# The scan's decay, spreading and carried products placed side by side in parts of TensorE's array, with banks in pairs for ScalarE and VectorE and new orders of the steps

## The reference

```python
h = _layernorm(h, ln_w, ln_b)
z, xBC, dt = split(h @ in_w.T, [512, 512 + 640])          # dt: 8 heads
dt = softplus(dt + dt_bias)
xBC = silu(causal_depthwise_conv(xBC, conv_w) + conv_b)   # 4 taps
x, B, C = split(xBC, [512, 576])                          # 8 heads x 64; state size 64
dA = exp(-exp(A_log) * dt)
# per token: state = dA * state + (dt * x) B^T ;  y = state C
y = y + D * x
y = y * silu(z)
y = y * rsqrt(mean(y * y) + EPS) * rms_w
h = res + y @ out_w.T
```

## Time and profile before

| | us |
|---|---|
| median of three runs | 1965.81 |
| the profiled execution | 1965.04 |
| its span in the trace | 1963.3 |
| TensorE busy | 1815.8 |
| VectorE busy | 1445.5 |
| ScalarE busy | 1309.1 |
| GpSimd busy | 1173.3 |

### The profile page before, as it was taken

The page is one execution under the profiler, slowest core; times in us unless marked ns, Lnnn a source line. Parts: engine busy times, 40 slices in busy tenths (PEclk is TensorE's granted clock), DMA queues, the critical chain, the costliest instruction groups (busy, mean ns, idle before and its releaser), DMA issues. The chain is left out here.

```text
span 1963.3 us, 36509 instructions
## 1 busy us (share of the span) xinstructions
PE 1815.8 (92%) x12544; PEld 1378.9 (70%) x12544; DVE 1445.5 (74%) x3135; ACT 1309.1 (67%) x2317; POOL 1173.3 (60%) x1032
## 2 busy tenths in 40 slices
PE   5799999999999999999999999999986589899998
PEld 4577777677777777776777777767754478777786
DVE  4687788887877777777777777777743586878755
ACT  3677767777677767677767776777640467676675
POOL 2466666666666654555555555555540487877785
PEclk8899999999999999999999999999986799999999
DMA  4011111111111111111111111110104202121001
GB/s 142 23 38 39 39 37 48 59 37 43 37 37 37 37 39 38 44 58 47 43 37 37 37 37 37 48 59 27 33 12 149 86 1 92 38 76 55 22 22 44
DMA packets 87272, 91.97 MB, mean 47 GB/s; under 512 B 4928, under 2 KB 82448, under 8 KB 87184
## 3 DMA queue, kind: packets, MB, share of 16 engines
q1 hardware_dynamic: 79360, 79.46, 12.5%
q10 hardware_dynamic: 7824, 11.37, 2.4%
HBM read 57.26 MB, written 25.17 MB: 42 GB/s over the span
## 5 line engine op out<-in xcount | busy, mean ns | idle before, releaser
L860 POOL TENSOR_TENSOR L_xc<-L_xpad,L_vec 128x512 f32<-128x512 f32 x160 | 165.9, 1037 | 421.2 <-ACT L_xpad L659 394.0
L381 PE MATMUL L_front<-L_uhi,L_whi 128*128 128x512 f32 x576 | 247.2, 429 | 13.1 <-DVE L_xc L1078 8.4
L530 PE MATMUL L_mix<-L_wo,L_yg 128*128 128x256 f32 x1024 | 238.4, 387 | 3.2 <-POOL L_yg L852 3.2
L381 PE MATMUL L_front<-L_uhi,L_wlo 128*128 128x512 f32 x576 | 229.5, 398 | 0.0
L381 PE MATMUL L_front<-L_ulo,L_whi 128*128 128x512 f32 x576 | 229.5, 398 | 0.0
L1090 DVE TENSOR_TENSOR L_m<-L_dbank,L_gm 128x512 f32<-128x512 f32 x256 | 175.5, 686 | 69.0 <-ACT L_dbank L699 68.6
L530 PEld LDWEIGHTS L_mix<-L_wo,L_yg 128*128 128x128 f32 x1024 | 191.8, 192 | 34.7 <-issue 7.0
L852 POOL TENSOR_TENSOR L_yg<-L_yg,L_sz 128x512 f32<-128x512 f32 x128 | 164.0, 1281 | 86.1 <-DVE L_yg L1105 86.1
L659 ACT ACTIVATE L_xpad<-L_front,L_pbias 128x512 f32<-128x512 f32 x160 | 108.7, 680 | 132.4 <-PE L_front L381 131.6
L697 ACT ACTIVATE L_dbank<-L_dbank 128x512 f32<-128x512 f32 x256 | 148.8, 581 | 45.5 <-PE L_dbank L437 45.4
L487 PE MATMUL L_ybank<-L_m,L_dtx 128*64 128x128 f32 x2048 | 161.3, 284 | 5.5 <-DVE L_m L1090 5.5
(11 more groups left out here) (172 smaller groups left out, 4850.3 us busy)
## 6 DMA issues: line engine op xcount, KB each, us to landing
h<-L_hres SPq DMA_DIRECT2D x32, 512.0 KB, 3.0
L_hin<-in_x SPq DMA_DIRECT2D x16, 512.0 KB, 4.6
L_hres<-in_x SPq DMA_DIRECT2D x16, 512.0 KB, 3.8
L_cc<-L_xc ACTq DMA_DIRECT2D x64, 128.0 KB, 2.3
L_hin<-h SPq DMA_DIRECT2D x16, 512.0 KB, 4.7
L_hres<-h SPq DMA_DIRECT2D x16, 512.0 KB, 3.7
M_hin<-h SPq DMA_DIRECT2D x16, 512.0 KB, 4.7
M_xin<-in_x SPq DMA_DIRECT2D x16, 512.0 KB, 5.7
```

The costliest lines, as they stand in the source:

```text
L381: last = nc.tensor.matmul(to[:, :], ww[:, kd, tile * P:(tile + 1) * P], a[:, kd, :], start=i == 0, stop=i == len(passes) - 1)
L530: last = nc.tensor.matmul(mix[1 - s][:, (b % 2) * DM:(b % 2 + 1) * DM], yg[:, t, b * P:(b + 1) * P], wo[layer][:, t, :], start=t == 0, sto ...
L860: nc.gpsimd.tensor_tensor(xc[p][:, q, :].rearrange("p (b i) -> p b i", b=NB), xpad[:, q, :, 0:P], vector(layer, "conv_w", q * TAPS, 1).uns ...
```

## The change

The two decay banks become one tensor `dbank` of two banks, and the two `mix` banks are views of one tensor `both`.

- `decays(n, k)`, k = 0 to 3 over pair of sequences and half of the heads, makes two products: the pair's two sequences lie in different rows of the array and go to different banks. `exp_decay` and `weigh` then take both banks (1024 columns) in one instruction.
- `carry(n, pair)` makes four products of 64 rows by 64 columns, in four quarters of the array; `exp_carry` and `scale_c` take both banks in one. To suit this, the halves of `cs`, `sdecay` and `state` hold the heads in another order (`on_half`: heads 0, 3 of each four in the lower partitions, 1, 2 in the upper), and `sel` shrinks to 64 columns.
- `outputs(n, p, pair)` makes two output tiles: `within` of both, then `carried` of both, in which four consecutive products (two tiles by odd and even head) lie in four quarters of the array and, by row, in different banks.
- The step sizes' weights get a tensor `wdt` of their own with both parts beside each other, 16 output rows: four products instead of six; `bias_dt` adds the two parts in two instructions.
- `step` is written anew for TensorE, ScalarE, GpSimd and VectorE.
- `clear_halo`'s wait moves to `set_halo`.

```diff
             def project_dt(n):
...
-                passes = [(kd, a, ww) for kd in range(KD) for ww, a in ((whi, uhi), (whi, ulo), (wlo, uhi))]
-                for i, (kd, a, ww) in enumerate(passes):
-                    last = nc.tensor.matmul(front[0][0:NH, :], ww[:, kd, NPROJ - NH:NPROJ], a[:, kd, :],
+                passes = [(kd, a) for kd in range(KD) for a in (uhi, ulo)]
+                for i, (kd, a) in enumerate(passes):
+                    last = nc.tensor.matmul(front[0][0:2 * NH, :], wdt[:, kd, :, :].rearrange("p i h -> p (i h)"), a[:, kd, :],
...
-            def decays(n, q):
-                b, half = q // 2, q % 2
+            def decays(n, k):
+                pair, half = k // 2, k % 2
...
-                wait(pe, m_done, 8 * n + q - 1)
-                rows = slice(ROWS * (b % 2), ROWS * (b % 2) + ROWS)
-                nc.tensor.matmul(dbank[half][:, :], dstat[rows, b // 2, :],
-                                 dmov[rows, b // 2, 4 * half:4 * half + 4, :], start=True, stop=True).then_inc(d_ready, 1)
+                wait(pe, m_done, 4 * n + k)
+                for i in range(2):
+                    rows = slice(ROWS * i, ROWS * i + ROWS)
+                    last = nc.tensor.matmul(dbank[:, i, :], dstat[rows, pair, :], dmov[rows, pair, 4 * half:4 * half + 4, :], start=True, stop=True)
+                last.then_inc(d_ready, 1)
...
+            def carry(n, pair):
+                scaled_x, kept_b, scaled_c = known(pe, NB * n + 4), known(pe, n + 1), known(pe, 2 * n + 1)
+                pe.wait_ge(consts_ready, 3)
+                if pair == 0:
+                    pe.wait_ge(dtx_done, scaled_x)
+                    pe.wait_ge(bt_done, kept_b)
                 else:
+                    pe.wait_ge(cs_done, scaled_c)
+                moving = dmov[:, pair, :, :].rearrange("r (k f) i -> r k f i", f=4)
+                for half in range(2):
+                    for i in range(2):
+                        rows = slice(ROWS * i, ROWS * i + ROWS)
+                        last = nc.tensor.matmul(mix[i][HD * half:HD * half + HD, :], sel[rows, :], moving[rows, :, on_half(half), :],
+                                                start=True, stop=True)
                 last.then_inc(ec_ready, 1)
...
             def carried(n, p, t, b):
                 for odd in range(2):
                     half = slice(HD * odd, HD * odd + HD)
-                    made = nc.tensor.matmul(ybank[t % 2][half, b * P:(b + 1) * P], state[p][half, b, t, :], cs[half, b, t, :],
+                    rows = slice(HD, 2 * HD) if (odd + t) % 2 else slice(0, HD)
+                    made = nc.tensor.matmul(ybank[t % 2][half, b * P:(b + 1) * P], state[p][rows, b, t, :], cs[rows, b, t, :],
...
+            def outputs(n, p, pair):
+                first, second = 2 * pair, 2 * pair + 1
+                if pair == 0:
+                    pe.wait_ge(m_done, 4 * n + 4)
+                for t in (first, second):
+                    wait(pe, y_skip, T * n + t - 1)
+                    for b in range(NB):
+                        within(n, t, b)
+                if pair == 0:
...
+                for b in range(NB):
+                    last_first = carried(n, p, first, b)
+                    last_second = carried(n, p, second, b)
+                last_first.then_inc(y_ready, 1)
+                last_second.then_inc(y_ready, 1)
...
+            def exp_decay(n, k):
+                act.wait_ge(d_ready, 4 * n + k + 1)
+                nc.scalar.activation(dbank[:, :, :], dbank[:, :, :], ACT.Abs).then_inc(d_abs, 1)
+                act.wait_ge(d_abs, 4 * n + k + 1)
+                nc.scalar.activation(dbank[:, :, :], dbank[:, :, :], ACT.Exp, scale=-1.0).then_inc(d_exp, 1)
...
+            def scale_c(n, pair):
+                dve.wait_ge(ec_exp, 2 * n + pair + 1)
+                of = cc[:, 2 * pair * P:(2 * pair + 2) * P].rearrange("p (b i) -> p b i", b=2)
+                nc.vector.tensor_tensor(cs[:, 2 * pair:2 * pair + 2, :, :], both[:, :, :].rearrange("p b (t i) -> p b t i", t=T),
+                                        of.unsqueeze(2).broadcast_to([P, 2, T, P]), ALU.mult).then_inc(cs_done, 1)
```

More of the change, by code:

```diff
@@ L40 @@
 NPROJ = 2 * DI + 2 * NS + NH
+NMAIN = NPROJ - NH
 SEQ, LEN = 8, 1024
@@ L241, in mamba_layers @@
         front = [bank(f"front{i}") for i in range(2)]
-        dbank = [bank(f"dbank{i}") for i in range(2)]
+        dbank = ctx.enter_context(nc.psum_tensor("L_dbank", [P, 2, 512], F32))
         ybank = [bank(f"ybank{i}") for i in range(2)]
-        mix = [bank(f"mix{i}") for i in range(2)]
+        both = ctx.enter_context(nc.psum_tensor("L_mix", [P, 2, 512], F32))
+        mix = [both[:, i, :] for i in range(2)]
         staged = m[:, :, :, :].rearrange("p b h i -> p (b h i)")[:, 0:C_END - C_MASK]
@@ L457, in turn_b @@
                 last.then_inc(bt_turned, 1)
[L459 to L464, removed]
-                else:
-                    pe.wait_ge(cs_done, NB * n + b - 1)
-                rows = slice(ROWS * (b % 2), ROWS * (b % 2) + ROWS)
-                moving = dmov[rows, b // 2, :, :].rearrange("r (t o) i -> r t o i", o=2)
-                for odd in range(2):
-                    last = nc.tensor.matmul(mix[b % 2][:, :], sel[rows, odd, :], moving[:, :, odd, :], start=odd == 0, stop=odd == 1)
+            def carry(n, pair):
[4 more added lines that the diff above has]
+                    pe.wait_ge(bt_done, kept_b)
+                else:
+                    pe.wait_ge(cs_done, scaled_c)
[5 more added lines that the diff above has]
+                                                start=True, stop=True)
                 last.then_inc(ec_ready, 1)
             def new_state(n, s):
-                pe.wait_ge(cs_done, NB * n + 3 + s)
+                pe.wait_ge(cs_done, 2 * n + 2)
                 pe.wait_ge(wx_done, NB * n + 2 * s + 2)
@@ L477, in new_state @@
                 for b in (2 * s, 2 * s + 1):
-                    values = wx[:, b, :, :].rearrange("p (t o) d -> p t o d", o=2)
-                    for odd in range(2):
-                        last = nc.tensor.matmul(mix[s][HD * odd:HD * odd + HD, (b % 2) * T * HD:(b % 2 + 1) * T * HD],
-                                                bt[:, b, :], values[:, :, odd, :], start=True, stop=True)
+                    values = wx[:, b, :, :].rearrange("p (k f) d -> p k f d", f=4)
+                    for half in range(2):
+                        last = nc.tensor.matmul(mix[s][HD * half:HD * half + HD, (b % 2) * T * HD:(b % 2 + 1) * T * HD],
+                                                bt[:, b, :], values[:, :, on_half(half), :], start=True, stop=True)
                 last.then_inc(st_ready, 1)
@@ L612, in step @@
                     fold_bias(layer_of(n, layer, 2))
+                result(n, layer, 0)
+                if more:
+                    decays(n + 1, 1)
                 if more2:
@@ L1225, in step @@
                     clear_halo(n, p)
-                skip(n, layer, p, 3)
                 if more:
-                    mask_scores(n + 1)
                     weigh(n + 1, 0)
-                    weigh(n + 1, 1)
                 if starts_layer(n + 2):
                     fold_rows(layer2)
+                mean_square(n)
                 if more2:
@@ L1235, in step @@
                     rest_u(n + 2, 1)
-                mean_square(n)
-                if more:
-                    weigh(n + 1, 2)
                 finish(n, layer, c, p, 0)
```

259 lines of the change are left out of this document (115 added, 144 removed).

## The result

The changed kernel takes 2000.61 us (median of 4 runs, 1999.91 to 2001.23), the kernel before 1965.87 beside it: ratio 1.0174, 95% interval 1.0162 to 1.0186. It is slower by 35 us. Forecast was 1909, and 2000.61 lies outside the range given. The profiled execution has a span of 1997.0 us against 1963.3.

The account below looks back on a forecast made before the run. TensorE was taken as the bound, with VectorE limiting the gain: 43.90 us per item to 42.1, 31x1.8 = 55.8 saved. 1965.0-55.8+1.4 (border)-2 (first and last item) = 1908.6, so 1909 us; range 1882 to 1948.

Parts of the forecast that it names:

- The rates: Times per product or operation on TensorE, VectorE and ScalarE, such as 0.12 us per four carried products.
- rival 1: TensorE's array quarters don't run side by side: no faster than two products per 0.11 us, about 1961 us; 7%.
- my floor of 41.4: Item time in us from laying rows end to end, without sum_da's last wait; 42.0 with it, 42.1 taken.
- the walk: One item's rows laid end to end in program order, each starting when engine and operand are free: 42.0 us.
- my own count of TensorE alone: TensorE's item without its waits: 43.9-0.85-4.8 = 38.3 us.
- Of 4.8 us some 1.8 are left: Of TensorE's 4.8 us relief per item, 1.8 shorten the item; the rest turns into waits for VectorE.
- the path: The new order of one item across the engines, pieces end to end with their waits, ending at 42.0 us.
- finish_dt to 38.2, so sum_da waits 0.6: Late in the item VectorE ends the step sizes at 38.2 us, so TensorE's sum_da waits 0.6.
- GpSimd's moved work (decay_state, ...) fits in its free 14 us: On GpSimd, decay_state, sums of squares and layer_norm ahead of the second tap fit in 14 free us per item.
- rival 3: Granted clock falls inside items where TensorE waits 1 us at a time: 45.3 us per item, 2008 us; 4%.
- the longer wait of the bias products (1.4): At the layer border, bias products ahead of result wait for ssq 2.7 us instead of 1.33: +1.4 once.
- A price of 0.46 per us of low clock: On TensorE each us of low clock costs 0.46; 7 us per item cost 3.2.

Follow-up runs that it names:

- both repairs: Changed kernel with finish_dt ahead of skip 0 and, at the layer border, fold_bias behind result half 0 and decays 1: 1873.46 us, ratio 0.953.
- the first experiment: Changed kernel with one move, VectorE's finish_dt ahead of skip 0 instead of behind skip 1, where GpSimd is idle: 1885.2 us, ratio 0.958.
- the filled wait: Changed kernel with four extra unused products on TensorE in front of its wait for da: 1950.88 us, ratio 0.9916.

## Why the prediction was wrong

*What held.* The rates. Two decay products at once, 0.39; four spreading products within 0.41; carried products start four within 0.02 us and the next four 0.109 later (taken: 0.12), so rival 1 is out. ScalarE's 1024-wide Exp takes 1.008 us (1.0), VectorE's product 1.223 (1.21). TensorE waits 1.04 for the last weighting (1.3), 1.03 for a convolution (0.95), 0.2 for the step sizes (0.3). One wait I had not seen: 0.57 for keep_b's copy ahead of the spreading. With the hold removed the item takes 40.95 us against my floor of 41.4 without the last wait and 42.1 with it: the walk was 0.45 too slow. Its waits are 1.07, 1.0, 0.6 and 0.17, 2.84 in all, against 2.75 forecast (0.3+0.2+0.95+1.3), so the 0.45 lies in TensorE's own pieces, which I laid end to end too long: 41.4 less 2.75 is 38.65, although my own count of TensorE alone was 38.3. Measured, less the waits, it is 38.1. "Of 4.8 us some 1.8 are left" was too little: 2.95 were to be had.

The Trainium skill, "TensorE: Matmul & The Clock Gate", section "Wait — 56ns, not 53.3ns?", gives about 62 ns per matmul where the sequencer decodes in software. By that figure the 32 recorded carried products would take 2.0 us, an estimate. They took 1.03, so that bound doesn't show here.

*The step that failed first* is in the path: "finish_dt to 38.2, so sum_da waits 0.6". It rests on "GpSimd's moved work (decay_state, ...) fits in its free 14 us", which stands ahead of it. I weighed the moved decay_state by its time on GpSimd alone and looked for who depends on it. Nobody does, at that place; it costs through contention. finish_dt's second product has both inputs in SBUF, and it takes 1774 ns beside decay_state's 1.90 us, 0.19 alone. From the walk, finish_dt had about 1.05 us: skip, two convolutions and skip take 34.4 to 37.15, and it ends at 38.2. It began on time (402.70, 2.8 us behind the start of skip 0) and took 2.5, to 405.23; so the wait became 2.0 instead of 0.6. The profile of before held the clue: L998, 128x32 elements, has a mean of 648 ns, and its neighbour of the same size 216. I did not ask why two equal sizes stood so far apart; it ended with GpSimd's first tap already then. The same slip sits behind decay_state's new place: what a moved instruction runs beside is part of its price.

*The step that failed second* is rival 3, to which I gave 4%. Its direction came (1.7% slower; it said 2008), its reason only in part. I let the clock fall over a stretch of 1 us waits and named 4 us of low clock per item as the point from which it decides. In the changed kernel it falls behind the one wait of 2.0 us, there are 3.4 us of low clock per item, and they cost 1.63 on top of the 1.99 of the hold. Waits of 1 us alone let it fall too, as the rival said, but only here and there: in 3 of 29 items with both repairs, in none of the first experiment's. What I held against it, the MLP at 1.00 with TensorE busy for 93%, says nothing of single waits: in the first layer's scan of the kernel before, TensorE's longest wait is 0.8 us, so no row of it showed what follows a wait of 2. The kernel before with an added wait (1.4 to 1.7 us, 95% busy, clock falling in 16 of 29 items) shows that a high busy share doesn't protect. A price of 0.46 per us of low clock was about right: 3.4x0.46 = 1.56.

*The border.* I counted the longer wait of the bias products (1.4) and nothing behind them. But result, the second decays and, through ScalarE's Exp of those, the folding of the new layer's weights stand in line: 3.05 for ssq, then at low clock 7.81 for the bias products and 6.74 for result, then 7.14 for the weights: +14.5 against before. Moving the bias products back gives 16.6.

*The sum made again.* 30 intervals at 44.57-40.95 are 109 us, the hold and its clock. 2000.6-109 = 1892, and the border of the first experiment is another 6.4 shorter (62.53): 1885, as measured. So even without the hold 1909 would have been 24 us too high: 42.1 was forecast for the item's 40.95, and the border's lengthening, forecast as 1.4, is 62.53-54.43 = 8.1.

What stays open: why the clock falls in some items and not in others after the same waits (28 of 29 items at 2.0 us, 14 of 29 at 1.4, 16 of 29 at 1.4 to 1.7 in the kernel before), and what lets it fall in some items at the earlier place, behind 0.56 and 1.03 us: in 3 of 29 with both repairs, 6 with the filled wait, 9 where the carried products stand apart, none in the first experiment.

## What to carry to other kernels

When an instruction moves, write down what will run beside it on the neighbouring engine, not only who depends on it; a small VectorE product with two SBUF inputs on the critical path belongs where GpSimd is idle, and a duration out of line with its size in the groups by form is the sign that it is not. Price a wait of TensorE twice: its own length, and low clock behind it; a 2 us wait here cost 3.6. At a seldom passed place such as a border of layers, follow the chain of everything that is queued behind the moved work, since here one early wait of 3.05 us stood in front of the bias products, result, the decays and the new weights.

## What the runs showed of the hardware

VectorE's products with two SBUF inputs are held to the end of an instruction of GpSimd that ran when they started: L_da 1774 ns beside 1.90 us, 1160 beside 1.26, 192 beside none. The bf16 mask product of 128x1024 does the same: 1.41 us beside GpSimd's gate in the changed kernel, 0.68 in the first experiment. Not every instruction of GpSimd holds them: beside the 1.01 us of L812, with 128x4 elements, L_da took 0.19 in the kernel before. L1117, which reads one operand from PSUM, is not held; VectorE's view of line L1117 gives least, median and longest of 128 in ns (one of them, at 412.11, starts while GpSimd's gate of 411.63 runs, and takes 0.74):

```profile
L1117 DVE SCALAR_TENSOR_TENSOR L_yg<-L_xc,L_vec,L_ybank x128: 736/745/749, 88.2 to 1497.7; 128x512 f32<-128x512 f32 x128
```

The Trainium skill, "GPSIMD Engine Reference", section "1. Specifications", says that the SBUF interfaces are shared with VectorE and that there is contention with its instructions that have two SBUF inputs. The runs agree and add the size: the wait is for the end of GpSimd's instruction, even where VectorE's own work is 0.19 us. They also show the exception of the 128x4 instruction.

TensorE does 32 recorded products of 64x64 with 128 columns, four quarters side by side, in 1.03 us with the change of shape, each with its own weight load: 0.109 per four. One tile after another they take 1.52.

The granted clock fell to the lower level for 3.4 us, in a few items 6.8, behind one wait: of 2.00 us in 28 of 29 items, of 1.4 in 14 of 29, of 1.4 to 1.7 in the kernel before in 16 of 29. In items whose waits were 1.07, 1.0, 0.6 and 0.17 it stayed at 1.00 in all 29 of the first experiment, and fell in 3 of 29 with both repairs.
